# A graph layer and a mixture of experts on one core: search rounds in two of three slots, weight pieces, row copies and first marks moved

## The chip, the cores and the metric

The kernel runs on 1 core of one Trainium2 chip. The metric is the device time of that core in microseconds, launch to end, of one execution. Only the order of the work changes, not what is computed.

## What is computed

The input is x (4096 rows of 128) and a dense float32 matrix adj (4096 by 4096), most of whose entries are 0. In short:

```python
# graph part; n = layernorm(x)
filt = tanh(adj * adj) * (adj > 0)
new_adj = filt with only the 350 largest entries of each row kept
h2 = tanh(n @ W_proj + b_proj)
x = x + relu(new_adj @ (h2 @ W_gcn) + b_gcn)
# expert part; n = layernorm(x), E = 8 experts, the 2 best per row
scores = n @ Wg.T + bg
probs = softmax(the 2 highest scores)
x = x + sum over those 2 experts e of probs * (relu(n @ W1[e].T + b1[e]) @ W2[e].T + b2[e])
```

Hidden width is 512. Only few rows of adj have more than 350 positive entries; the kernel counts the positive entries of every row, corrects up to four rows among the first 512 early on, and has a general repeat for the rest that is skipped when the counts ask for none.

## The kernel before, in words

Each of the five engines (SP, POOL = GpSimd, DVE = VectorE, ACT = ScalarE, PE = TensorE) has a program of its own, written out by hand in the order in which it runs; semaphores join them. An engine that waits holds everything behind the wait.

**The stream.** adj is read in 64 chunks of 1 MB (NCH), eight (NK) for each of the eight blocks of 512 rows of the result (NB, IW). SP issues the loads (line 450) into four buffers; the load of chunk n waits until ScalarE has squared chunk n - 4 and VectorE has marked it (s_sq, s_raw, lines 448 and 449). ScalarE squares (line 1235) and takes tanh (1239), TensorE multiplies with g_sb (1487), VectorE counts positive entries with mark_positive (lines 939 to 950; even chunks write marks, odd ones add). Each engine's program has one slot n for each chunk, 65 in all (FFN). Other work is put into slots by number.

**The start.** VectorE normalises x in eight groups of 512 rows (normal_group, 760), TensorE turns them, projects them, ScalarE applies tanh into g_sb. POOL waits for all eight groups (644), then loads the first four pieces of the expert weights and prepares constants.

**The weights.** W2 and W1 come in eight pieces each. VectorE splits a piece into two float16 halves (split_piece, 959) in the slot that WAT (58) gives. For W1, POOL first loads a piece and its last row (first_pair, 593) and subtracts (take_last_row, line 605); staging has room for two such pairs, so each pair waits for the split of an earlier one. bias_row (690) puts the bias in after the last split.

**The early search.** For up to four rows of block 0 with more than 350 entries the 350th largest value is found in 15 rounds (STEPS), one in each of slots 20 to 34 (STEP0). A round is count_candidates (797) on VectorE, a matmul (1412) on TensorE, and raise_threshold (807) on VectorE in the next slot. Before it a row of flags goes out and back by DMA (1318, 786), the rows are fetched (394) and squared (793). In slot TIE (35) and after, ties are counted and the rows corrected; write_features (836) is in slot 42.

**The routing.** A finished block b = ORDER[i] is routed from slot START[i] on, each step at an offset: add_features (856) at +1, normalise (869) and cut_rows (880) at +2, transposes on TensorE and copy_norm on ScalarE (1276) at +3, the gate and choose (893) at +4, choose_second (905) and exp_diff (1285) at +5, places (1466), probabilities (913) and assign (921) at +6. Then POOL scatters the block's rows to DRAM by expert with eight indirect DMAs (scatter, 697, issue in 709). It waits for the cut, the copy, the probabilities and the assignment. POOL's program has the scatters in order, one behind the other, with no slot numbers.

**The experts.** SP waits for the end of the stream's use of abuf, for the scatters of the first six blocks (516, 517) and for the tile table of first_tiles (1022), which is made in slot FIRST (58); then it loads 256-row tiles by transposing DMAs (469, 471) into abuf. TensorE works on 36 tiles (layer1 and layer2, 1563 and 1581), ScalarE and VectorE in between (1334, 1136, 1342, 1144), POOL scatters the results (727). The blocks i = 6 and 7 are still being routed beside the first tiles; slot 65 is tile 0. At the end the results are read back, added and stored.

## Time and profile before

| | us |
|---|---|
| median of 3 runs | 498.88 |
| lowest, highest | 494.01, 499.02 |
| the profiled execution | 498.55 |
| its span, first to last instruction | 496.8 |
| TensorE busy | 405.6 (82%) |
| VectorE busy | 361.9 (73%) |
| ScalarE busy | 324.0 (65%) |
| POOL busy | 224.5 (45%) |

The stream takes about the first 309 us of the span, the experts the time to about 474, the last reading, adding and storing the rest. The busy shares are averages over these stages; they don't say what sets the end of one. For that one reads a table by stage, and then the waits.

### The profile page before, as it was taken

How to read it: one execution, taken by the hardware profiler on the slowest of the kernel's cores; microseconds unless marked ns; L12 is line 12 of the kernel's file. 1: busy time of each engine (PE TensorE's matmuls, PEld its weight loads, DVE VectorE, ACT ScalarE, POOL GpSimd, SP SyncE). 2: the span in 40 equal slices, each digit the busy share in tenths (PEclk: the TensorE clock that was granted, in tenths of full speed). 3: DMA queues.
4: the chain of work that ended last, by engine and by line, in shares of the span. 5: the costliest groups of instructions: out<-in, count | busy, mean ns of one | idle time of the engine just before them, and what ended most of it. 6: DMA issues, size and time to landing. Idle time of an engine off the chain costs nothing.

```text
span 496.8 us, 7360 instructions
## 1 busy us (share of the span) xinstructions
PE 405.6 (82%) x2144; PEld 232.5 (47%) x2144; DVE 361.9 (73%) x952; ACT 324.0 (65%) x329; POOL 224.5 (45%) x315
## 2 busy tenths in 40 slices
PE   2896999989889899999999999588578779687600
PEld 2453533334434334544554444466357668576500
DVE  4999958678999999969799998296356545354326
ACT  4577999899678879999998995153144344253300
POOL 7249965240217008144054883644744545535510
PEclk9998999989799999999999999888879999988955
DMA  8629889894658568776766982622234333210059
GB/s 277 245 97 413 334 278 324 304 353 150 245 214 252 194 222 296 294 292 240 289 214 239 312 301 49 107 54 56 98 96 88 85 56 78 63 40 30 22 177 335
DMA packets 54898, 97.08 MB, mean 195 GB/s; under 512 B 34165, under 2 KB 41386, under 8 KB 46658
## 3 DMA queue, kind: packets, MB, share of 16 engines
q1 hardware_dynamic: 43584, 79.40, 47.7%
q0 software_dynamic: 6560, 14.88, 9.6%
q10 hardware_dynamic: 4706, 2.23, 1.5%
q8 instruction: 21, 0.34, 0.3%
q14 instruction: 27, 0.22, 0.1%
HBM read 80.00 MB, written 12.27 MB: 186 GB/s over the span
## 4 chain that ended last, share of the span: by engine, by line
PE 43%; DVE 23%; issue 10%; ACT 9%; another core or an unknown queue 7%; DMA 6%; SPq 1%; ACTq 1%; POOL 0%; POOLq 0%; DVEq 0%
PE bank L1487 23%; ACT tbuf L1235 5%; PE bank L1601 5%; DVE marks L950 3%; PE bank L1602 3%; PE bank L1575 2%; PE bank L1577 2%; PE bank L1576 2%; DVE marks L947 2%; DMA tbuf<-expert_rows 2%; DVE rowbf L802 2%; DVE tbuf L1136 2%; DMA xres<-in_x 2%; DVE abuf L1144 1%
## 5 line engine op out<-in xcount | busy, mean ns | idle before, releaser
L1487 PE MATMUL bank<-tbuf,g_sb 128*128 128x512 f32 x512 | 242.4, 619 | 8.3 <-ACT g_sb L1249 5.2
L1487 PEld LDWEIGHTS bank<-tbuf,g_sb 128*128 128x128 f32 x512 | 95.6, 197 | 115.1 <-issue 98.9
L1235 ACT ACTIVATE tbuf<-abuf 128x2048 f32<-128x2048 f32 x64 | 121.5, 1898 | 13.1 <-DMA abuf<-in_adj_tiles 10.4
L1239 ACT ACTIVATE tbuf<-tbuf 128x2048 f32<-128x2048 f32 x64 | 122.3, 1911 | 2.0
L709 POOL DMA_INDIRECT routed_rows<-aug,slots x64 | 79.1, 1236 | 79.9 <-DVE base L930 62.0
L727 POOL DMA_INDIRECT expert_rows<-abuf,xmeta x72 | 70.5, 979 | 73.0 <-DVE abuf L1144 58.5
L950 DVE SCALAR_TENSOR_TENSOR marks<-abuf,marks 128x2048 bf16<-128x2048 int32 x32 | 76.4, 2387 | 1.6 <-DMA abuf<-in_adj_tiles 0.5
L1136 DVE SCALAR_TENSOR_TENSOR tbuf<-bank,tbuf 128x512 f16<-128x512 f32 x72 | 46.9, 682 | 37.2 <-ACT tbuf L1334 19.9
L1601 PE MATMUL bank<-w2hl,tbuf 128*128 x288 | 58.1, 288 | 15.5 <-issue 10.8
L1334 ACT ACTIVATE tbuf<-bank 128x512 f16<-128x512 f32 x72 | 41.0, 605 | 44.7 <-remote 27.3
L1602 PE MATMUL bank<-w2hl,tbuf 128*128 x288 | 54.4, 228 | 8.5 <-issue 8.5
L1342 ACT ACTIVATE abuf<-bank,xmeta 128x128 f32<-128x128 f32 x72 | 23.0, 371 | 53.8 <-remote 33.2
L1144 DVE SCALAR_TENSOR_TENSOR abuf<-bank,xmeta,abuf 128x128 f32<-128x128 f32 x72 | 22.0, 343 | 40.0 <-ACT abuf L1342 34.7
L1575 PE MATMUL bank<-abuf,w1h 128*128 128x256 f16 (+1 forms) x160 | 43.6, 275 | 4.6 <-issue 4.1
L1577 PE MATMUL bank<-abuf,w1l 128*128 128x256 f16 (+1 forms) x160 | 43.6, 275 | 3.5 <-issue 3.5
L1576 PE MATMUL bank<-abuf,w1h 128*128 128x256 f16 (+1 forms) x160 | 43.6, 275 | 1.8 <-issue 1.8
L947 DVE TENSOR_SCALAR marks<-abuf 128x2048 bf16<-128x2048 int32 x32 | 42.9, 1340 | 0.1
L1601 PEld LDWEIGHTS bank<-w2hl,tbuf 128*128 128x128 f16 x288 | 29.5, 103 | 21.8 <-issue 17.2
L1602 PEld LDWEIGHTS bank<-w2hl,tbuf 128*128 128x128 f16 x288 | 29.5, 103 | 14.4 <-issue 14.1
L1575 PEld LDWEIGHTS bank<-abuf,w1h 128*128 x160 | 16.4, 103 | 10.3 <-issue 7.6
L598 POOL DMA_DIRECT2D wstage<-in_w x8 | 5.8, 728 | 32.5 <-DVE w1l L973 32.2
L1577 PEld LDWEIGHTS bank<-abuf,w1l 128*128 x160 | 16.5, 103 | 5.6 <-issue 3.7
(250 smaller groups left out, 438.0 us busy)
## 6 DMA issues: line engine op xcount, KB each, us to landing
abuf<-in_adj_tiles SPq DMA_DIRECT2D x64, 1024.0 KB
wstage<-in_w POOLq DMA_DIRECT2D x24, 256.0 KB, 6.4
tbuf<-expert_rows SPq DMA_DIRECT2D x8, 512.0 KB, 7.2
out<-xres ACTq DMA_DIRECT2D x8, 256.0 KB, 6.2
routed_rows<-pad SPq DMA_DIRECT2D x9, 130.0 KB
expert_rows<-abuf,xmeta POOLq DMA_INDIRECT x72
routed_rows<-aug,slots POOLq DMA_INDIRECT x64
abuf<-routed_rows SPq DMA_TRANSPOSE x40
```

The lines of the kernel that those rows point to most:

```text
L709: pool.indirect_dma_start(xs, bass.IndirectOffsetOnAxis(ap=slots[:, q, k * SUB + cc:k * SUB + cc + 1], axis=0), aug[:, q, k, cc, :], None) ...
L727: pool.indirect_dma_start(ys, bass.IndirectOffsetOnAxis(ap=xmeta[:, t % NT, s, 0:1].bitcast(i32), axis=0), ysb[:, u, s, :], None, bounds_c ...
L950: dve.scalar_tensor_tensor(mark, bits_in, 1.0, mark, ALU.min, ALU.add).then_inc(s_raw, 1)
L1136: dve.scalar_tensor_tensor(hl[:, q, hb, :].rearrange("p h s -> p (h s)"), ps_h(q, half)[:, :], 0.0, hh[:, q, hb, :].rearrange("p h s -> p ...
L1235: act.activation(tbuf[:, n % NBUF, :, :], abuf[:, n % NBUF, :, :], ACT.Square).then_inc(s_sq, 1)
L1239: act.activation(tbuf[:, n % NBUF, :, :], tbuf[:, n % NBUF, :, :], ACT.Tanh).then_inc(s_t, 1)
L1487: last = pe.matmul(ps_feat[ib % 2][:, :], g_sb[:, c, :], tbuf[:, buf, cc, :], start=(c == 0), stop=(c == C - 1))
L1575: pe.matmul(dst, hi, xhl[:, u, 0, rows], start=True, stop=False)
L1576: pe.matmul(dst, hi, xhl[:, u, 1, rows], start=False, stop=False)
L1577: last = pe.matmul(dst, lo, xhl[:, u, 0, rows], start=False, stop=True)
L1601: pe.matmul(y_bank(t, s), hs, hi_lo, start=False, stop=False, skip_group_check=True)
L1602: last = pe.matmul(y_part(t, s, 0), ls, hi, start=False, stop=(hb == HB - 1), skip_group_check=True)
```

## The change

The search runs in two of every three slots from 20 to 41 (SEARCH) instead of in each of 20 to 34, so TIE moves from 35 to 42 and what hangs on it by 7. W1's pieces are split in slots 10, 12, 14, 16, 18 and 44, 46, 48 instead of 11, 13 ... 25; POOL loads the last pair, and puts in the bias row, between the scatters of i = 2 and i = 3. START[4] and START[5] move from 47 and 51 to 50 and 54, and with the latter FIRST from 58 to 61. On ScalarE the copy of the cut rows becomes copy_rows at +5 (it stood with copy_norm at +3), the exponential moves from +5 to +6 and the probabilities from +6 to +7; the last block keeps +3, +5 and +6. The marks of chunks 0 to 3 are made between x's last groups (0 and 1 after group 4, 2 after group 5, 3 after group 6), and POOL's wait for the groups asks for five instead of eight.

```diff
--- before.py
+++ after.py
@@ -55,23 +55,26 @@
     NTA = NT
     PW = 512
     NPC = E * H // PW
-    WAT = [2 + i if i < NPC else 11 + 2 * (i - NPC) for i in range(2 * NPC)]
+    WAT = [2 + i for i in range(NPC)] + [10, 12, 14, 16, 18, 44, 46, 48]
     NCH = NB * NK
 
 
     ORDER = list(range(1, NB // 2 + 1)) + [0] + list(range(NB // 2 + 1, NB))
-    START = [19, 27, 35, 43, 47, 51, 58, 65]
+    START = [19, 27, 35, 43, 50, 54, 58, 65]
 
     AT_ADD, AT_NORM, AT_TURN, AT_COPY, AT_GATE = 1, 2, 3, 3, 4
-    AT_CHOOSE, AT_SECOND, AT_EXP, AT_PLACE, AT_PROB, AT_ASSIGN = 4, 5, 5, 6, 6, 6
+    AT_CHOOSE, AT_SECOND, AT_PLACE, AT_ASSIGN = 4, 5, 6, 6
+
+    AT_ROWS, AT_EXP, AT_PROB = ([s] * (NB - 1) + [e] for s, e in ((5, 3), (6, 5), (7, 6)))
     OUT = 1
     MARKS = 4
     GROUPS = 4
     TOTAL = 3
     FIX = NK + TOTAL + 2
     STEP0 = FIX + 7
-    TIE = STEP0 + STEPS
+    SEARCH = [STEP0 + 3 * b // 2 for b in range(STEPS)]
+    TIE = SEARCH[-1] + 1
     FFN = NCH + 1
 
     COUNT = 14
@@ -641,7 +644,7 @@
             for b in range(STEPS):
                 for k in range(4):
                     pool.memset(bits[:, b, k:k + 1], k << (2 * (STEPS - 1 - b)))
-            pool.wait_ge(s_xn1, NK)
+            pool.wait_ge(s_xn1, NK - 3)
             for i in range(4):
                 load_weights(i)
             pool.memset(pad[:, :, :], 0.0)
@@ -713,12 +716,15 @@
             unit_column()
             first_pair(0)
             first_pair(1)
-            for j in range(NPC):
+            for j in range(NPC - 1):
                 take_last_row(j)
-                if j + 2 < NPC:
+                if j + 2 < NPC - 1:
                     first_pair(j + 2)
-            bias_row()
             for i, b in enumerate(ORDER):
+                if i == 4:
+                    first_pair(NPC - 1)
+                    take_last_row(NPC - 1)
+                    bias_row()
                 if i:
                     scatter(i - 1, routed)
             def store_tile(t, u):
@@ -760,16 +766,6 @@
                     ins = dve.tensor_scalar(xnorm[g % XG][:, c % CK, 0:D - 1], xres[:, c, 0:D - 1], mean[:, c:c + 1],
                                             rstd[:, c:c + 1], ALU.subtract, ALU.mult)
                 ins.then_inc(s_xn1, 1)
-
-            for i, (c0, c1) in enumerate(PIECES):
-                dve.wait_ge(s_x[i], 16)
-                for c in range(c0, c1):
-                    last = dve.bn_stats(stats[:, c, :], xres[:, c, :])
-                link(last)
-                link(norm_scale(dve, link, c0, c1 - c0))
-                for g in range(c0 // CK, c1 // CK):
-                    normal_group(g)
 
             CHAIN = 2 + 4 * STEPS + 1 + 4 + R
             TOTS = STEPS + 1
@@ -1067,10 +1063,10 @@
 
             def ready_steps(n):
 
-                if STEP0 < n <= TIE:
-                    raise_threshold(early, 0, n - STEP0 - 1)
-                if STEP0 <= n < TIE:
-                    count_candidates(early, 0, n - STEP0)
+                if n - 1 in SEARCH:
+                    raise_threshold(early, 0, SEARCH.index(n - 1))
+                if n in SEARCH:
+                    count_candidates(early, 0, SEARCH.index(n))
                 if n == TIE:
                     count_ties(early, 0)
                 for i, b in enumerate(ORDER):
@@ -1087,14 +1083,27 @@
                         cut_rows(i, routed)
                     if n == START[i] + AT_CHOOSE:
                         choose(i, b, routed)
-                    if n == START[i] + AT_PROB:
+                    if n == START[i] + AT_PROB[i]:
                         probabilities(i, routed)
                     if n == START[i] + AT_ASSIGN:
                         assign(i, routed)
+
+            FIRST_MARKS = {NK - 4: (0, 1), NK - 3: (2,), NK - 2: (3,)}
+            for i, (c0, c1) in enumerate(PIECES):
+                dve.wait_ge(s_x[i], 16)
+                for c in range(c0, c1):
+                    last = dve.bn_stats(stats[:, c, :], xres[:, c, :])
+                link(last)
+                link(norm_scale(dve, link, c0, c1 - c0))
+                for g in range(c0 // CK, c1 // CK):
+                    normal_group(g)
+                    for n in FIRST_MARKS.get(g, ()):
+                        mark_positive(n)
+
             for n in range(FFN):
                 ready_steps(n)
-                if n < NCH:
+                if NBUF <= n < NCH:
                     mark_positive(n)
                 for i in range(2 * NPC):
                     if n == WAT[i]:
@@ -1274,11 +1283,13 @@
 
             def copy_norm(i, rs):
-                q = i % 2
                 act.wait_ge(rs.r2, i + 1)
                 if i:
                     act.wait_ge(rs.r3, i)
                 act.activation(xnt[:, :], space(i).xn[:, :], ACT.Copy).then_inc(rs.xt, 1)
+
+            def copy_rows(i, rs):
+                q = i % 2
                 act.wait_ge(rs.cut, 2 * i + 2)
                 act.activation(aug[:, q, 1, :, 0:D], aug[:, q, 0, :, 0:D], ACT.Copy).then_inc(rs.ax, 1)
 
@@ -1295,7 +1306,9 @@
                 for i in range(NB):
                     if n == START[i] + AT_COPY:
                         copy_norm(i, routed)
-                    if n == START[i] + AT_EXP:
+                    if n == START[i] + AT_ROWS[i]:
+                        copy_rows(i, routed)
+                    if n == START[i] + AT_EXP[i]:
                         exp_diff(i, routed)
 
             for n in range(FFN):
@@ -1358,6 +1371,7 @@
                     relu_rows(general, r)
                 for i in range(NB):
                     copy_norm(i, rerouted)
+                    copy_rows(i, rerouted)
                     exp_diff(i, rerouted)
                 for t in range(NT, 2 * NT):
                     relu_h(t, t % 2)
@@ -1487,8 +1501,8 @@
                     last = pe.matmul(ps_feat[ib % 2][:, :], g_sb[:, c, :], tbuf[:, buf, cc, :],
                                      start=(c == 0), stop=(c == C - 1))
                 last.then_inc(s_pe, 1)
-                if STEP0 <= n < TIE:
-                    total_candidates(early, 0, n - STEP0)
+                if n in SEARCH:
+                    total_candidates(early, 0, SEARCH.index(n))
 
             def pair_counts(m):
```

## Rows read from the trace of the kernel before

**Rows 1.** Stages: each engine's busy us (instructions), TensorE's granted clock, DMA share, GB/s.
```profile
60.00:110.00 50.00, 47.27 (x129) 19.27 (x130) 35.22 (x43) 47.01 (x28) 23.50 (x32) 0.97 0.88 312
110.00:190.00 80.00, 72.20 (x243) 33.29 (x242) 74.21 (x199) 64.81 (x42) 20.82 (x22) 0.96 0.63 217
190.00:308.00 118.00, 117.21 (x477) 56.60 (x476) 105.62 (x300) 109.88 (x78) 55.96 (x48) 1.00 0.74 258
...
302.00:304.00 2.00, 2.00 (x6) 0.93 (x6) 1.73 (x9) 1.97 (x2) 0.13 (x1) 1.00 0.35 66
308.00:324.00 16.00, 10.90 (x88) 7.85 (x87) 4.64 (x12) 4.03 (x9) 7.69 (x8) 0.85 0.57 93
```
The columns are PE, PEld, DVE, ACT and POOL in this order.

**Rows 2.** Waits of VectorE from 110 to 308 us: us in total, times, longest.
```profile
DVE scores L895 <- PE bank L1463: 1.9, 2, 1.7
DVE okc L809 <- PE bank L1412: 1.6, 1, 1.6
```

**Rows 3.** Timeline of POOL: start, us, what, idle before it and its releaser.
```profile
31.97 2.59 POOL L590 DMA_DIRECT2D wstage<-in_w  x4 [16.80 <-DVE aug L760]
...
109.98 1.26 POOL L605 TENSOR_TENSOR wstage<-wstage 128x512 f32<-128x512 f32 x1
...
271.62 1.67 POOL L709 DMA_INDIRECT routed_rows<-aug,slots  x1 [5.36 <-DVE base L930]
...
286.88 0.98 POOL L709 DMA_INDIRECT routed_rows<-aug,slots  x1 [0.28 <-POOL aug L701]
...
296.83 1.61 POOL L709 DMA_INDIRECT routed_rows<-aug,slots  x1 [0.30 <-issue]
...
310.91 0.98 POOL L709 DMA_INDIRECT routed_rows<-aug,slots  x1 [8.78 <-DVE base L930]
```

**Rows 4.** Timeline of SP's queue at its first tile load.
```profile
301.11 1.33 SPq L469 DMA_TRANSPOSE abuf<-routed_rows  x1
```

**Rows 5.** Timeline of TensorE at its first tile.
```profile
309.72 0.28 PE L1575 MATMUL bank<-abuf,w1h 128*128 128x256 f16 x1
```

**Rows 6.** Timeline of VectorE: start, us, what.
```profile
28.53 1.10 DVE L760 TENSOR_SCALAR xnt<-xres,moments,rstd 128x127 f32<-128x127 f32 x4
...
110.31 2.02 DVE L947 TENSOR_SCALAR marks<-abuf 128x2048 bf16<-128x2048 int32 x1
...
133.76 0.42 DVE L971 TENSOR_SCALAR w1h<-wstage 128x512 f16<-128x512 f32 x1
...
134.82 0.18 DVE L895 TENSOR_TENSOR scores<-bank,gate_b 128x32 f32<-128x32 f32 x1
...
150.10 0.14 DVE L809 SCALAR_TENSOR_TENSOR okc<-bank,cand 128x4 f32<-128x4 f32 x1
...
151.74 2.28 DVE L950 SCALAR_TENSOR_TENSOR marks<-abuf,marks 128x2048 bf16<-128x2048 int32 x1
...
284.79 0.15 DVE L1018 TENSOR_TENSOR tiles<-base,base_i 1x8 f32<-1x8 f32 x1
...
288.36 2.27 DVE L950 SCALAR_TENSOR_TENSOR marks<-abuf,marks 128x2048 bf16<-128x2048 int32 x1
...
300.86 1.22 DVE L947 TENSOR_SCALAR marks<-abuf 128x2048 bf16<-128x2048 int32 x1
...
305.27 2.29 DVE L950 SCALAR_TENSOR_TENSOR marks<-abuf,marks 128x2048 bf16<-128x2048 int32 x1
```

**Rows 7.** Timeline of ScalarE at the square of chunk 4.
```profile
38.71 1.91 ACT L1235 ACTIVATE tbuf<-abuf 128x2048 f32<-128x2048 f32 x1 [4.26 <-DMA abuf<-in_adj_tiles]
```

**Rows 8.** Waits of VectorE from 40 to 110 us.
```profile
DVE top L786 <- DMA b_f<-key: 3.9, 1, 3.9
DVE rowval L793 <- DMA rowval<-in_adj_rows: 3.1, 1, 3.1
```

**Rows 9.** Chain of waits from 38 to 60 us: start, us, what.
```profile
43.10 3.48 PE bank L1487 x4
...
47.47 1.72 PE bank L1487 x4
```

## The prediction, made before the changed kernel was run

> **What bounds the kernel now.** I read the stages first [rows 1]. From 60 to 110 us ScalarE is busy 47.0 of 50 us and VectorE only 35.2: ScalarE sets the pace. From 110 to 190 VectorE has 74.2 of 80, TensorE 72.2, ScalarE 64.8. From 190 to 308 TensorE shows 117.2 of 118, and VectorE 105.6. That looks as if VectorE had room for more work in the last stretch, but its busy time leaves out the short pauses between linked instructions. So I read its waits next [rows 2]: in the 198 us from 110 to 308 it waits for another engine about 3.5 us in all (1.9 for the gate scores, 1.6 for a count total). VectorE is therefore full from slot 20 to slot 63, and TensorE is nearly full beside it in the second part. A slot is one chunk of the adjacency matrix; its number can be counted off by the marks.
>
> At the hand-over to the experts I read the queues. SP can issue the first tile load only when the scatter of the sixth routed block (i = 5) has landed: the scatter's last issue is at 296.83 and takes 1.61, and SP's first transpose is at 301.11 [rows 3, 4], 2.7 us behind it. TensorE starts the first tile at 309.72 [rows 5], straight after the stream. So the loads are some 5 us ahead of need today, and that cushion is what the change touches.
>
> **The change, part by part.**
>
> *First marks earlier.* Normalising a group takes 1.10 us with a pitch near 1.0 [rows 6]. Chunk 0's mark moves ahead of three groups, so chunk 4's load starts 3 us earlier; ScalarE sat 4.26 us waiting for it [rows 7]. The work of VectorE is only reordered, and TensorE turns group 5 long after it is ready, so the cover holds. POOL's weight loads, which waited 16.80 us until 31.97 for the last group [rows 3], also go 3 us earlier. But what follows passes through a chain with fixed latencies: the flag row is written and read back (VectorE waits 3.9), then four adjacency rows are fetched (3.1) [rows 8]. The key is ready only after slot 13 on VectorE. In slot 10 W1's first piece now stands before the bias: it waits for POOL, which I place 3 us earlier than today, and mark 11 comes some 2 us later than today; slots 11 to 13 make that good, as one split and the bias no longer stand there. I leave 0.7 us of the 3 for the key and all behind it. Bounds: 3 us gained, or 1 us lost if POOL does not come earlier.
>
> *W1's pieces.* One piece costs 134.82 - 133.76 = 1.1 us [rows 6]. The fifth moves from slot 19 to slot 18, into the 3.1 us wait for the rows: 1.1 gained ahead of slot 20. POOL's subtraction at 109.98 ran against mark 20, which took 2.02 where such a mark takes 1.22 [rows 3, 6]: 0.8 gained, as this subtraction now runs in the slack before. The subtraction for the seventh piece leaves the full stretch too; I give it the same 0.8. Pieces six to eight (3.2 us) stay inside the full stretch, only later. On POOL's queue the last pair of loads (two transfers of 256 KB), its subtraction and the bias row's two transfers move behind the scatter of block i = 2 and ahead of that of i = 3, which waits for slot 50 anyway; their 0.5 MB are small beside the 258 GB/s that the stream moves there [rows 1]. The split in slot 48 waits for that subtraction. I expect POOL to be done about 1 us before; if not, VectorE waits one for one, and with it all marks behind.
>
> Here a rule bears on the sum. The row shows 2.02 against 1.22 for the mark beside POOL's subtraction [rows 3, 6]. The Trainium skill ("SBUF — State Buffer", "SBUF: two separate sides") says that VectorE and GpSimd take one port pair as an exclusive lock, and that the loser stands still for the whole instruction. By this rule the same collision comes back wherever the last subtraction lands, and one of the two gains of 0.8 falls away if the moved subtraction meets a mark again: 500.6 instead of 499.8. The trace agrees for this pair.
>
> *Early search.* One round (raise, count) is 151.74 - 150.10 = 1.64 us [rows 6]. Slots 20 to 34 had 15 rounds and now have 10: 8.2 us and with pieces six to eight 11.4 us leave these slots. All of it comes back in slots 35 to 48. As VectorE waits for almost nothing in either part [rows 2], a shift inside a full engine's queue gains nothing by itself. It can gain only the 3.5 us of waits. The bounds are 3.5 gained, and 3.5 lost where rounds and routing now meet TensorE too early. I take 2 gained: TensorE runs ahead more evenly, but a round still needs its chunk's matmuls.
>
> *ScalarE's copies apart.* The row copy and the exponential stand one to two slots later. ScalarE no longer holds its chunks for them; it was not the bound behind slot 20, so nothing by itself. But the probabilities move from +6 to +7, and a scatter waits for them: every scatter but the last starts one slot later. For the first five nobody is waiting. For i = 5 SP is.
>
> *START 47 and 51 become 50 and 54; the tile table with them (58 to 61).* Block i = 5's places were ready in slot 57, and its scatter queued behind i = 4's. Now its probabilities come at the end of slot 61, where before 300.86 stood [rows 6]. The tile table (288.36 - 284.79 = 3.6 us [rows 6]) then lies behind them, not before.
>
> **The sum.** Slot 20 starts at 110.3 - 0.7 - 1.1 - 0.8 = 107.7. From there to the probabilities of i = 5 VectorE has what it did in 300.86 - 110.31 = 190.55, less the table 3.6, less one collision 0.8, less 2 of waits: 184.2, so 291.9. The scatter: today's last one took 298.44 - 286.88 = 11.6; eight times 0.98 and 0.30 is 10.2 at best, and the one before it took 286.88 - 271.62 = 15.3 [rows 3]. I take 11.6, the nearest in place and neighbours: 303.5. Landing and SP's start 2.7: 306.2. Between 302 and 304 the DMA moved 66 GB/s [rows 1], about one tile of 128 KB in 2 us, so the first tile is there about 3 us after SP's start: 309.2, against 309.72 today: 0.5 earlier. VectorE finishes mark 63 at 291.9 + 3.6 + (307.6 - 300.9) = 302.2, where it ended near 307.6, so the stream does end 5 us sooner; but TensorE then stands idle some 6 us. After such a pause it ran at 1.2 GHz: four of the same matmuls took 3.48 us after a pause and 1.72 a moment later [rows 9]. That costs 1.7 (0 to 1.7). Together 1.2 us later at the experts, and the rest of the kernel follows: its scatter of i = 6 now waits for VectorE's first tile (near 313 instead of 310.91 [rows 3]) but has slack before the last loads. The profiled execution took 498.55 us with a span of 496.8; plus 1.2 gives **499.8 us**. Its own time is 0.3 under the median 498.88, so against the median the forecast is +0.9 us, 0.2%: no change. About 1% (5 us) is what this kernel's runs can tell from none, since its three runs spread from 494.01 to 499.02.
>
> **Rivals.**
> *Slower, 505 us.* The scatter of i = 5 becomes the late step. Its place is the end of slot 61; its price is one for one to the first tile. If POOL brings the eighth piece late, or the rounds wait for TensorE, the 2 us of waits do not go; with a scatter of 15.3 instead of 11.6 it is 2 + 3.7 = 5.7 more: 505.5. It decides from the point where the probabilities of i = 5 end after 295.5. For it speaks that a step ahead of SP moved four slots back; against it that VectorE gains 2.6 us before slot 20.
> *Faster, 492 us.* All 3.5 us of waits go (1.5 more), the start keeps 3 us instead of 0.7 (2.3 more), the scatter takes 10.2 (1.4 more), TensorE keeps its clock (1.7): 499.8 - 6.9 = 492.9. Beside it: after the first tiles TensorE is busy only 10.9 of 16 us [rows 1]; if the pause ahead of the experts takes the place of part of these 5.1 us instead of adding to them, 1 to 3 us more go. For it speaks that the work of that stretch is the same and now starts with an idle engine; against it that the scatter of i = 6 and the tile loads still run in it.
> *It doesn't do what it says, 498.5 us.* The early marks gain nothing behind the key chain, the search only changes places in a full queue, and the cushion before the first tile absorbs the later scatter exactly. No step moves the end.
>
> **Chances.** Forecast 0.40 (its own range 495 to 504), nothing moves 0.10, faster 0.30, slower 0.20. The likeliest is 499.8. The range from 492 to 505.5 leaves out the tails beyond either rival's sum, about 2 in 10. Faster by over 1% 0.30, within 1% 0.50, slower 0.20.
>
> **What would show it.** Right: mark 20 near 107.7; mark 35 over 10 us earlier than today, yet the mark of slot 63 only about 5 us earlier; VectorE without waits in between; SP's first transpose near 306 and TensorE idle 5 us or more before its first tile. Wrong: mark 63 earlier by more than 8 us (VectorE was not full); SP starting before 303; a wait of VectorE for POOL's subtraction in slot 48; TensorE's first tile following the stream at once.

## The result, and the profile after

The changed kernel takes 502.31 us (median of 4 runs, 500.72 to 503.01) against 496.44 us of the kernel before in the same session (4 runs, 493.45 to 499.02): the ratio is 1.0116, 95% interval 1.0074 to 1.0157. The forecast was 499.8 us, no change; the change is slower by 1.2%. The number lay in the range, 2.5 us above the forecast. But the call of "no change", which stood for less than 1%, was wrong: the change is slower, clear of noise, and by a little more than that 1%. The profiled execution took 502.0 us with a span of 500.2, 3.4 more than the span before; the medians differ by 5.9.

The page of the changed kernel, its second part (busy tenths in 40 slices of 12.5 us, granted clock) and the chain by engine:

```profile
PE   3999987999999999999999981858648798788500
...
PEclk9999997999999999999999995859959999979955
...
DVE 28%; PE 26%; issue 11%; POOL 10%; DMA 10%; another core or an unknown queue 7%; ACT 4%; SPq 2%; ACTq 1%; DVEq 1%; POOLq 0%
```

Slice 24 of PE (from 300 us) is where a 9 became a 1, and PEclk has a 5 there. That is the hand-over to the experts. The stages of [rows 1] again, from 110 us on, same columns:

```profile
110.00:190.00 80.00, 78.29 (x273) 35.81 (x273) 74.47 (x204) 78.00 (x50) 24.25 (x21) 1.00 0.71 255
190.00:308.00 118.00, 107.73 (x450) 51.91 (x448) 102.38 (x297) 97.07 (x71) 50.91 (x47) 0.98 0.65 229
302.00:304.00 2.00, 0.62 (x4) 0.11 (x4) 1.79 (x6) 0.00 (x0) 1.70 (x2) 0.57 0.10 33
308.00:324.00 16.00, 11.11 (x88) 9.36 (x89) 5.49 (x18) 3.61 (x7) 5.04 (x6) 0.75 0.47 76
```

From 110 to 190 us TensorE is busy 78.3 of 80 us, where it had 72.2: the stream runs ahead. From 302 to 304 it had 2.00 and has 0.62, and from 308 to 324 its mean clock fell from 0.85 to 0.75. In the chain POOL has 10% where the kernel before had 0%, and PE 26% where it had 43%: the scatter, once beside the work, is now part of what sets the end. What was gained in the stream is lost at its end.

VectorE's waits from 40 to 110 us (us in total, times, longest), answering to [rows 8]:

```profile
DVE w1h L967 <- POOL wstage L608: 8.1, 1, 8.1
DVE top L782 <- DMA b_f<-key: 5.7, 1, 5.7
DVE rowval L789 <- DMA rowval<-in_adj_rows: 0.9, 1, 0.9
```

and from 110 to 305, answering to [rows 2]:

```profile
DVE w1h L967 <- POOL wstage L608: 1.9, 1, 1.9
DVE aug L884 <- issue: 1.6, 1, 1.6
DVE okc L805 <- PE bank L1426: 1.5, 3, 0.6
DVE scores L891 <- issue: 1.3, 1, 1.3
DVE feat_t L837 <- issue: 0.5, 1, 0.5
```

The start has a new wait of 8.1 us for GpSimd's first subtraction; a wait of 5.7 us of the bias for TensorE, which the kernel before has at 71.76, is gone. For the full stretch [rows 2] shows only part of the waits of the kernel before. These two belong to it as well:

```profile
DVE feat_t L841 <- issue: 2.9, 1, 2.9
DVE place L924 <- PE bank L1473: 0.8, 1, 0.8
```

So VectorE waited 7.2 us before and waits 6.8 now: nearly the same, yet the stretch is shorter.

The hand-over, engine by engine. VectorE's timeline: the row cut of block i = 6, the probabilities of i = 5, and the last mark of the stream.

```profile
288.70 0.43 DVE L884 CAST aug<-nrm 128x508 f16<-128x508 f32 x1 [1.56 <-issue]
...
292.45 0.17 DVE L915 TENSOR_TENSOR aug<-ex,aug 128x4 f32<-128x4 f32 x1
...
300.12 2.29 DVE L946 SCALAR_TENSOR_TENSOR marks<-abuf,marks 128x2048 bf16<-128x2048 int32 x1
```

POOL's timeline: the moved subtraction, then the first and the last of the eight issues of scatter i = 5.

```profile
232.83 1.27 POOL L608 TENSOR_TENSOR wstage<-wstage 128x512 f32<-128x512 f32 x1 [7.48 <-DMA wstage<-in_w]
...
293.49 0.99 POOL L712 DMA_INDIRECT routed_rows<-aug,slots  x1 [6.93 <-DVE aug L915]
...
304.83 0.97 POOL L712 DMA_INDIRECT routed_rows<-aug,slots  x1 [0.30 <-issue]
```

SP's first transpose, answering to [rows 4]:

```profile
308.46 1.32 SPq L472 DMA_TRANSPOSE abuf<-routed_rows  x1
```

TensorE: the last matmul group of the stream, the first tile's first three matmuls, the second tile's first, answering to [rows 5]:

```profile
302.46 0.62 PE L1518 MATMUL bank<-marks,ones_bf 128*32 128x512 bf16 x4 [1.53 <-DVE marks L946]
311.98 0.39 PE L1589 MATMUL bank<-abuf,w1h 128*128 128x256 f16 x1 [8.90 <-DMA xmeta<-routed_rows]
312.16 0.42 PE L1590 MATMUL bank<-abuf,w1h 128*128 128x256 f16 x1
312.37 0.42 PE L1591 MATMUL bank<-abuf,w1l 128*128 128x256 f16 x1
...
316.30 0.27 PE L1589 MATMUL bank<-abuf,w1h 128*128 128x256 f16 x1
```

Read them as one chain: probabilities end at 292.62, scatter from 293.49 to 305.80, SP at 308.46, first tile at 311.98. TensorE has nothing to do from 303.1 on. Before, the tile stood at 309.72 straight behind the stream. It is 2.3 us later now, and the second tile, at 312.15 before, is 4.15 us later, since TensorE comes back at half clock. The matmuls of the first tile follow each other in 0.21 us; in the kernel before it was 0.11:

```profile
309.84 0.27 PE L1576 MATMUL bank<-abuf,w1h 128*128 128x256 f16 x1
309.95 0.27 PE L1577 MATMUL bank<-abuf,w1l 128*128 128x256 f16 x1
```

The granted clock from 312 to 314 us is 0.50 where it was 1.00, the 1.2 GHz level instead of 2.4.

### The profile page after: what moved, and what is told of

It is laid out like the page before. It is cut to its first block, busy times and chain, and to the rows that moved or that the text cites. A ratio compares the mean times of both kernels' runs of the same rounds, so it can differ in the third digit from the quotient of the medians.

```text
span 500.2 us, 7361 instructions
## 1 busy us (share of the span) xinstructions
PE 401.0 (80%) x2144; PEld 230.2 (46%) x2144; DVE 360.7 (72%) x952; ACT 324.0 (65%) x329; POOL 224.8 (45%) x315
## 4 chain that ended last, share of the span: by engine, by line
DVE 28%; PE 26%; issue 11%; POOL 10%; DMA 10%; another core or an unknown queue 7%; ACT 4%; SPq 2%; ACTq 1%; DVEq 1%; POOLq 0%
PE bank L1501 10%; DVE marks L946 6%; POOL routed_rows L712 6%; PE bank L1615 4%; DVE marks L943 3%; DMA wstage<-in_w 3%; DMA xres<-in_x 3%; PE bank L1591 3%; PE bank L1589 2%; DVE tbuf L1145 2%; DMA tbuf<-expert_rows 2%; PE bank L1590 2%; PE bank L1616 2%; ACT tbuf L1244 2%
## 5 line engine op out<-in xcount | busy, mean ns | idle before, releaser
L1501 PE MATMUL bank<-tbuf,g_sb 128*128 128x512 f32 x512 | 237.7, 610 | 4.2 <-ACT g_sb L1258 2.8
L1501 PEld LDWEIGHTS bank<-tbuf,g_sb 128*128 128x128 f32 x512 | 94.4, 194 | 108.9 <-issue 98.2
L712 POOL DMA_INDIRECT routed_rows<-aug,slots x64 | 81.1, 1267 | 112.3 <-DVE aug L915 76.4
L1615 PE MATMUL bank<-w2hl,tbuf 128*128 x288 | 56.7, 285 | 6.1 <-issue 4.0
L1616 PE MATMUL bank<-w2hl,tbuf 128*128 x288 | 53.6, 227 | 8.6 <-issue 8.5
L943 DVE TENSOR_SCALAR marks<-abuf 128x2048 bf16<-128x2048 int32 x32 | 41.3, 1291 | 0.2
L1589 PEld LDWEIGHTS bank<-abuf,w1h 128*128 x160 | 16.3, 102 | 21.4 <-issue 18.9
L608 POOL TENSOR_TENSOR wstage<-wstage 128x512 f32<-128x512 f32 x8 | 14.3, 1784 | 18.1 <-DMA wstage<-in_w 18.0
```

The lines of the kernel that those rows point to most:

```text
L712: pool.indirect_dma_start(xs, bass.IndirectOffsetOnAxis(ap=slots[:, q, k * SUB + cc:k * SUB + cc + 1], axis=0), aug[:, q, k, cc, :], None) ...
L943: dve.tensor_scalar(mark, bits_in, 1.0, None, ALU.min).then_inc(s_raw, 1)
L1501: last = pe.matmul(ps_feat[ib % 2][:, :], g_sb[:, c, :], tbuf[:, buf, cc, :], start=(c == 0), stop=(c == C - 1))
L1589: pe.matmul(dst, hi, xhl[:, u, 0, rows], start=True, stop=False)
L1615: pe.matmul(y_bank(t, s), hs, hi_lo, start=False, stop=False, skip_group_check=True)
L1616: last = pe.matmul(y_part(t, s, 0), ls, hi, start=False, stop=(hb == HB - 1), skip_group_check=True)
```

## The experiments

There are twelve runs, in three groups; each ratio is against runs of the kernel before beside it. The first two groups ran on chips on which the kernel before takes 450 us, the last on one where it takes 497. Up to the first tile the timelines agree between them to about 2 us; the difference lies in the experts' phase (last section). So ratios are compared throughout, and times of the trace up to the first tile.

"Mark n" is the start of VectorE's mark of chunk n. Each such time comes from one execution, and executions of the same code differ: the six traces with the changed kernel's start have mark 20 between 108.55 and 110.46. A difference of less than 2 us between two traces proves little; the ratios rest on more executions.

### The anchors

**changed_again**: the changed kernel, unedited.

> The changed kernel, nothing edited, on the chip of the other runs of this group: the anchor for them. The hand-over theory expects the same timeline up to the hand-over as in its first profile (mark 63 near 300, SP's first transpose near 308.5, first tile near 312) and slower than the kernel before by 1 to 1.5%. If the loss belonged to the experts' phase of the first chip, where 14 tiles took 45 us longer than here, it would now be within 0.5% of the kernel before.

Measured: ratio 1.0121 [1.0086, 1.0156]. Mark 63 at 299.49, SP at 307.97, first tile at 311.83, span 454.3. The loss is the same 1.2% on a chip whose experts' phase is 47 us shorter, so it doesn't come from what is particular to the first chip.

**before_again**: the kernel before, unedited.

> The kernel before, nothing edited, on the same chip, for its trace: mark 63 near 305, SP's first transpose near 301, first tile near 309.7 or, if this chip's stream ends earlier, straight after it; its time is that of the kernel before.

Measured: ratio 0.9993 [0.9969, 1.0017], span 448.7. Mark 63 at 306.66, SP at 303.32, first tile at 311.12 straight behind the stream.

These two traces are the cleanest pair. Stages of the kernel before (columns as in [rows 1]), then of the changed one:

```profile
300.00:311.00 11.00, 11.00 (x42) 5.22 (x40) 9.11 (x23) 6.37 (x7) 3.37 (x3) 1.00 0.26 48
311.00:318.00 7.00, 7.00 (x71) 6.31 (x68) 4.74 (x11) 3.85 (x9) 4.48 (x5) 1.00 0.60 104
```

```profile
300.00:311.00 11.00, 0.70 (x8) 0.10 (x4) 3.16 (x6) 0.00 (x0) 4.77 (x5) 0.63 0.14 36
311.00:318.00 7.00, 6.17 (x35) 5.08 (x36) 1.81 (x5) 1.79 (x3) 0.71 (x1) 0.60 0.43 75
```

and TensorE's first and second tile in each, before first:

```profile
311.12 0.28 PE L1575 MATMUL bank<-abuf,w1h 128*128 128x256 f16 x1
...
313.54 0.27 PE L1575 MATMUL bank<-abuf,w1h 128*128 128x256 f16 x1
```

```profile
311.83 0.39 PE L1589 MATMUL bank<-abuf,w1h 128*128 128x256 f16 x1 [9.61 <-DMA xmeta<-routed_rows]
...
316.50 0.29 PE L1589 MATMUL bank<-abuf,w1h 128*128 128x256 f16 x1
```

The first tile is only 0.71 us later (311.83 against 311.12), but the second follows after 4.67 instead of 2.42: 2.25 us for half clock. Counting the tiles on, tile 24 starts 4.3 us later (387.7 against 383.4) and the span ends 5.6 us later. Of the 4.3 us only 0.7 are thus the later start. TensorE's mean clock from 310 to 418 us is 0.95 instead of 1.00: it is at half level in the first tile and again behind the gap that follows the fourth (granted clock 0.50 from 327 to 330 us, 1.00 in before_again, which has a gap there too). Why it falls in that gap in one kernel and not in the other is open. The last 1.3 us, behind the last tile, I can't name.

### The hand-over by itself

**before_block5_late**, on the kernel before:
```
-    START = [19, 27, 35, 43, 47, 51, 58, 65]
+    START = [19, 27, 35, 43, 47, 55, 58, 65]
```


> The kernel before, with block i = 5 started at slot 55 instead of 51, so that its probabilities stand in slot 61, where the changed kernel has them; nothing else differs. Theory A (the hand-over sets the start of the experts): TensorE's stream still ends near 308, but the scatter of i = 5 starts behind slot 61 (about 301 us), ends near 313, SP's first transpose comes near 316 and the first tile near 319 instead of 309.7: 505 to 508 us, slower by 6 to 9. Rival B (the loss lies in the search or in the later W1 pieces, and the cushion takes the late scatter): within 2 us of the kernel before.

Measured: 1.0352 [1.0325, 1.0379], 15 us. SP's queue, then TensorE's last group of the stream and its first tile:

```profile
319.70 1.32 SPq L469 DMA_TRANSPOSE abuf<-routed_rows  x1
```

```profile
314.99 0.40 PE L1504 MATMUL bank<-marks,ones_bf 128*32 128x512 bf16 x4 [1.44 <-DVE marks L950]
323.65 0.39 PE L1575 MATMUL bank<-abuf,w1h 128*128 128x256 f16 x1 [8.26 <-DMA xmeta<-routed_rows]
```

The cushion doesn't take the late scatter. Block i = 5's probabilities end at 304.1 here, and the first tile is 19.6 us behind. The cost was larger than expected (6 to 9): the probabilities came 3 us later than I had put them, so the first tile is 12.5 us later than in before_again (323.65 against 311.12), and the pause of 8.3 us adds its clock. VectorE's mark 63 came at 312.65 instead of 306.66, which I had not expected. Its waits tell where that comes from: from 110 to 315 us it waits 16.0 us for TensorE and the features' copy, where it waited 8.7 in before_again, and what came on top are waits for TensorE. The longest is 4.25 us for the gate's scores, at 290.89; in before_again its longest wait for TensorE is 1.8:

```profile
290.89 0.19 DVE L895 TENSOR_TENSOR scores<-bank,gate_b 128x32 f32<-128x32 f32 x1 [4.25 <-PE bank L1463]
```

Why TensorE has these results later was not traced.

**block5_one_slot_sooner**, on the changed kernel:
```
-    START = [19, 27, 35, 43, 50, 54, 58, 65]
+    START = [19, 27, 35, 43, 50, 53, 58, 65]
```


> The changed kernel with block i = 5 started at slot 53 instead of 54 and nothing else. Theory A: one slot is 4 us here, so the scatter ends near 302, SP starts near 304.5 and the first tile comes near 308: 3 to 4 us less, 498 to 499. Rival B: the block only changes places, same as the changed kernel within 1 us.

Measured: 1.0022 [0.9997, 1.0047], against 1.0121 of the changed kernel: 1% back, 4.5 us, as the hand-over says. SP at 303.60, first tile at 307.24; mark 63 (300.13) hasn't moved. One digit takes back the loss, up to the 0.5% that the interval leaves. Rival B is out.

**copies_together_again**, on the changed kernel:
```
-    AT_ROWS, AT_EXP, AT_PROB = (... ((5, 3), (6, 5), (7, 6)))
+    AT_ROWS, AT_EXP, AT_PROB = (... ((3, 3), (5, 5), (6, 6)))
```


> The changed kernel with ScalarE's row copy, exponential and the probabilities back at +3, +5 and +6 for every block; thin search and late blocks stay. Theory A: the probabilities of i = 5 stand one slot sooner (60), scatter ends near 302, first tile near 308: 3 to 4 us less than the changed kernel, as with block 5 one slot sooner. Rival B (ScalarE then holds its chunks back and TensorE's stream with them): mark 63 1 to 3 us later and the gain halved or gone.

Measured: 1.0005 [0.998, 1.0029], 1.2% back. SP at 302.52, first tile at 306.48, TensorE still waits 6.9 us for it. Mark 63 stands at 296.82, 2.7 us earlier than in the changed kernel, so this trace shows no sign that ScalarE's copies inside the chunks' way hold the stream back (rival B wanted it later). Part of that, 1.7 us, was there at mark 20 already (108.55 against 110.21), where nothing is edited.

**search_dense_again**, on the changed kernel:
```
-    START = [19, 27, 35, 43, 50, 54, 58, 65]
+    START = [19, 27, 35, 43, 47, 51, 58, 65]
-    SEARCH = [STEP0 + 3 * b // 2 for b in range(STEPS)]
+    SEARCH = [STEP0 + b for b in range(STEPS)]
```


> The changed kernel with the search back at one round per slot and the blocks i = 4 and 5 back at slots 47 and 51; early marks, W1's late pieces and the copies apart stay. Theory A: the probabilities of i = 5 come in slot 58, its scatter ends near 301, SP starts near 304, and the first tile follows the stream near 308 to 310: 497 to 499 us, 3 to 5 under the changed kernel. Rival B (W1's late pieces or the one-slot-later probabilities cost by themselves): stays at 501 to 503. Rival C (the thin search is what shortened the stream by 5 us): mark 63 ends near 305 again instead of 300.

Measured: 0.996 [0.9935, 0.9985]. The first tile (305.56) comes 3.6 us behind SP's first transpose and only 0.6 behind the stream. Mark 63 is at 300.99, where rival C wanted 305 and the changed kernel has 299.49: most of the stream's gain is not the thin search's. Blocks 4 and 5 moved in the same edit, so the two parts are not told apart here. No cost of W1's late pieces shows either.

The chain from the probabilities to the first tile can now be read from six traces in which TensorE waited for it over 4 us:

| kernel | probabilities of i = 5 end | SP's first transpose | first tile | sum |
|---|---|---|---|---|
| changed, first profile | 292.6 | 308.5 | 312.0 | 19.4 |
| changed_again | 292.0 | 308.0 | 311.8 | 19.8 |
| before_block5_late | 304.1 | 319.7 | 323.7 | 19.6 |
| block5_one_slot_sooner | 288.7 | 303.6 | 307.2 | 18.6 |
| copies_together_again | 285.1 | 302.5 | 306.5 | 21.4 |
| w1_odd_slots (below) | 290.0 | 306.0 | 309.5 | 19.6 |

(The last column is the distance from the probabilities to the first tile.) In copies_together_again the scatter alone, from its first issue to the end of its last, took 13.3 us, against 12.3 in the first profile. The first tile comes at the later of two: 18.6 to 21.4 us behind these probabilities, mostly 19 to 20, or the end of the stream.

### The start

**w1_odd_slots**, on the changed kernel:
```
-    WAT = [2 + i for i in range(NPC)] + [10, 12, 14, 16, 18, 44, 46, 48]
+    WAT = [2 + i for i in range(NPC)] + [11, 13, 15, 17, 19, 44, 46, 48]
```


> The changed kernel with W1's first five pieces back in slots 11, 13, 15, 17 and 19 instead of 10, 12, 14, 16 and 18. VectorE waited 8.1 us in slot 10 for GpSimd's first subtraction, so the theory that this wait ate what the early marks gained expects it to fall to about 5 us, mark 13 near 78 instead of 81 and mark 20 up to 1 us earlier or, with a piece in slot 19 and a collision beside mark 20, 1 us later. The hand-over theory expects the end to follow the probabilities of i = 5 one for one: within 1.5 us of the changed kernel either way. The rival (the start decides on its own) expects 3 us less.

Measured: 1.0105 [1.0079, 1.0132]. Mark 20 at 107.69; on the same chip two kernels with the changed kernel's start have it at 110.46 (block5_one_slot_sooner) and 108.96 (search_dense_again). First tile at 309.51, 2.3 earlier than in changed_again. The time's interval can't be told from the changed kernel's. VectorE's timeline here (bias, mark 11, W1's first piece, mark 13), then the changed kernel's:

```profile
65.41 0.28 DVE L974 TENSOR_SCALAR b_f<-bank 32x128 f32<-32x128 f32 x1
...
66.18 2.27 DVE L946 SCALAR_TENSOR_TENSOR marks<-abuf,marks 128x2048 bf16<-128x2048 int32 x1
74.20 0.43 DVE L967 TENSOR_SCALAR w1h<-wstage 128x512 f16<-128x512 f32 x1 [5.75 <-POOL wstage L608]
...
77.19 4.01 DVE L946 SCALAR_TENSOR_TENSOR marks<-abuf,marks 128x2048 bf16<-128x2048 int32 x1
```

```profile
73.78 0.43 DVE L967 TENSOR_SCALAR w1h<-wstage 128x512 f16<-128x512 f32 x1 [8.06 <-POOL wstage L608]
...
74.85 0.27 DVE L974 TENSOR_SCALAR b_f<-bank 32x128 f32<-32x128 f32 x1
...
75.61 2.27 DVE L946 SCALAR_TENSOR_TENSOR marks<-abuf,marks 128x2048 bf16<-128x2048 int32 x1
...
81.08 2.28 DVE L946 SCALAR_TENSOR_TENSOR marks<-abuf,marks 128x2048 bf16<-128x2048 int32 x1
```

The piece can be split at about 74 in both, because GpSimd's transfers and subtraction decide. With the piece in slot 10 the bias and mark 11, 3.1 us of work that needs nothing from GpSimd, queue behind the wait; with it in slot 11 they fill it. So mark 13 is at 77.2 instead of 81.1.

The other traces agree on mark 13 and less on what is left at mark 20. With the changed kernel's slots mark 13 stands at 80.6 to 81.5 (six traces), with slots 11, 13 and so on at 77.2 to 77.4 in three; a fourth, milder_search_copies_together, has 79.7, but its first mark was 2.4 us late already (29.20 against 26.79 in milder_search). At mark 20 it is 108.6 to 110.5 against 107.7 to 108.0 and, in the late trace, 110.66: 0.6 to 2.8 us, not 2.8 for certain.

**early_marks_alone**, on the kernel before (the old loop over x's pieces goes):
```
-            pool.wait_ge(s_xn1, NK)
+            pool.wait_ge(s_xn1, NK - 3)
...
+            FIRST_MARKS = {NK - 4: (0, 1), NK - 3: (2,), NK - 2: (3,)}
...
+                    for n in FIRST_MARKS.get(g, ()):
+                        mark_positive(n)
...
-                if n < NCH:
+                if NBUF <= n < NCH:
```


> The kernel before with only the early marks (chunks 0 to 3 marked between x's last groups, and the weight loads' wait three groups earlier). W1's order stays 11, 13, 15 and so on. By the prediction's step 0.7 us are left of three: first tile 0.7 earlier, within 0.3% of the kernel before. The runs so far (mark 20 at 107.7 to 107.9 with W1 in odd slots, 111.4 in the kernel before) say that over 2 us are left when the first piece of W1 does not wait: mark 20 near 108.5 to 109.5, first tile 2 to 3 us earlier, ratio 0.993 to 0.997.

Measured: 0.9949 [0.9919, 0.9978]. Mark 20 at 109.14 (110.31 in [rows 6]), mark 63 at 302.38 instead of 305.27, first tile at 306.84, 2.9 us earlier than in the first profile; the ratio says 2.5, with 1.1 to 4.0 in its interval. The early marks, together with the earlier weight loads, keep most of the 3 us of which I had left 0.7. At mark 20 only 1.2 us of it show; at mark 35 it is 2.9 (186.71 against 189.59 in the first profile). What gave the rest between the two was not looked into.

### The clock in the pause

**pause_filled**, on the changed kernel, ahead of the experts' tiles on TensorE:
```
+            for _ in range(42):
+                pe.matmul(bank[0][:, :], ones_bf[:, :], marks[:, 0, 0, :], start=True, stop=True)
```


> The changed kernel with 42 idle matmuls (128x512, their result is never read) on TensorE between its stream and the first tile, so that the pause of 9.6 us is filled without moving anything else. Theory: the granted clock stays at full, the first tile is followed by the second 2.4 us later as in the kernel before, where the changed kernel took 4.7, and the time falls by 2 to 3.5 us to 452 to 453.5, so that the pause costs its clock beside its length. Rival: the late loads set the second tile as well, and nothing moves.

Measured: 1.0097 [1.0061, 1.0133]; not told apart from the changed kernel. TensorE:

```profile
302.86 11.18 PE L1659 MATMUL bank<-marks,ones_bf 128*128 128x512 bf16 x42
313.88 0.27 PE L1589 MATMUL bank<-abuf,w1h 128*128 128x256 f16 x1
...
316.29 0.27 PE L1589 MATMUL bank<-abuf,w1h 128*128 128x256 f16 x1
```

The pitch to the second tile is 2.4 us instead of 4.3, as expected. But the idle matmuls ran partly at half clock themselves (granted clock 0.50 from 303 to 306 us, 0.86 from 306 to 309), took 11.2 us and ended about 2 us after the tile could have started: SP's first transpose was at 308.21, and the tile follows it by 3.5 in the first profile. Second tile at 316.29 against 316.30: the clock costs some 2 us at the second tile, and they are paid either way here. That a pause without this cost would also end the kernel earlier, the other half of the theory, this run doesn't show; my count of 42 was too high.

### Both gains without the loss

**dense_search_and_odd_w1**: search_dense_again with w1_odd_slots's line.

> The changed kernel with both undone: search one round per slot with blocks 4 and 5 at slots 47 and 51, and W1's first five pieces in slots 11, 13, 15, 17, 19. Early marks, W1's last three pieces late and the copies apart stay. Theory A (the first tile sets the end, and the two gains add up): mark 20 near 107 instead of 109, scatter of i = 5 ends near 297, first tile at the end of the stream near 303: 2 to 3 us under the dense search alone, 5 to 6 under the kernel before, 1.2%. Rival (the W1 order gains only where VectorE is the late one, and the stream of TensorE ends at the same time): as the dense search alone, 0.4% under the kernel before.

Measured: 0.9918 [0.9891, 0.9944]. Scatter i = 5 ends at 298.3, SP at 300.92, first tile at 304.46, 1.1 us earlier than in search_dense_again. The time is 0.4% (1.9 us) below that kernel's, where 2 to 3 us were expected, and the two intervals just overlap: that the gains add up is likely, but not clear of noise.

**milder_search**, on the one before:
```
-    SEARCH = [STEP0 + b for b in range(STEPS)]
+    SEARCH = [STEP0 + 5 * b // 4 for b in range(STEPS)]
```


> Built on dense_search_and_odd_w1: the search in four of five slots (20 to 37) instead of every slot, blocks 4 and 5 at 47 and 51. VectorE waited 3.2 us for the features' copy and 1.3 for the places with the dense search, which the thin one did not show. Theory: these waits go in part, mark 63 comes near 298.5 instead of 300, the first tile near 303 instead of 304.5, 1 to 1.5 us less: 444 to 445, ratio 0.987 to 0.991. Rival: the search only changes places in a full queue and the time stays at that of dense_search_and_odd_w1, 445.4.

Measured: **0.9829** [0.9786, 0.9873], 488.01 us where the kernel before takes 496.69. Mark 63 at 295.42 and TensorE without a pause:

```profile
298.87 0.62 PE L1518 MATMUL bank<-marks,ones_bf 128*32 128x512 bf16 x8
299.89 0.28 PE L1589 MATMUL bank<-abuf,w1h 128*128 128x256 f16 x1 [0.40 <-DMA xmeta<-routed_rows]
...
302.31 0.27 PE L1589 MATMUL bank<-abuf,w1h 128*128 128x256 f16 x1
```

That is better than the theory had it (mark 63 near 298.5). A search thinned just so far that it ends before slot 38 keeps block i = 4 at slot 47, and with it i = 5 at 51. The wait of 3.2 us for the features' copy is gone, as expected; the 1.3 for the places stayed. How much of the step from 0.9918 to 0.9829 is the search's stays open: the two ran on different chips, and dense_search_and_odd_w1 was not repeated on this one.

**milder_search_copies_together**: the same with the copies as in copies_together_again.

> milder_search with ScalarE's row copy, exponential and the probabilities back at +3, +5 and +6 for every block. Theory: the scatter of i = 5 starts one slot sooner, so SP is not late in any case, and the stream of VectorE alone sets the first tile: as milder_search or up to 1.5 us less (443 to 445). Rival: with the copies in the chunks' way ScalarE holds TensorE back and the stream ends 1 to 2 us later.

Measured: 0.9822 [0.9782, 0.9862], no different from milder_search. The trace looks otherwise: mark 63 at 299.82, first tile at 304.06, 4.2 us later than in milder_search. Of these 2.4 are there at the first mark, ahead of every edit; the other 1.8 are what the rival wanted (1 to 2 us), but the ratios don't show them, and their intervals are too wide to rule them out. So no effect of ScalarE's copies apart is shown once the hand-over isn't late, and milder_search's own 299.89 is the value of one execution, and one below the median (486.76 against 488.01). Both versions beat the two kernels.

## Why the prediction was right in part, and where it failed

*The start, 2.6 us earlier at mark 20 (107.7).* Wrong: 109.92, 0.4 earlier. One part is a slip in the sum: the collision of 0.8 lies inside mark 20, behind its start, so it belongs to the stretch that follows, and the mark should have been put at 108.5. The 291.9 isn't changed by it. Of the other terms, the early marks by themselves were undersized (0.7 was left; 1.2 at mark 20 and 2.9 at the first tile in early_marks_alone). I saw that the piece in slot 10 stands ahead of the bias and waits for GpSimd, and wrote that slots 11 to 13 make that good. They don't: one slot later, mark 13 comes 3.2 us or more earlier, and of this 0.6 to 2.8 are left at mark 20 (w1_odd_slots). So the rows for the search were ready at 105.17, 0.2 later than before, where I had them 0.7 earlier. The "1.1 gained" by the fifth piece was half there: from mark 19 to mark 20 it is 4.5 us instead of 5.1.

*The subtraction's collision.* With W1 in even slots it did go: mark 20 takes 1.22 instead of 2.02. That was partly luck, as before_block5_late, with the old slots, has 1.22 there too. The rule that I weighed against it is that of the Trainium skill ("SBUF — State Buffer", "SBUF: two separate sides"): VectorE and GpSimd hold one port pair in turn, and the loser stands still. Its size fits these pairs. In w1_odd_slots mark 13, from 77.19 on, took 4.01 us instead of 2.28 beside this row of POOL,

```profile
77.76 1.28 POOL L608 TENSOR_TENSOR wstage<-wstage 128x512 f32<-128x512 f32 x1
```

The mark ended at 81.20, which is, to 0.1, its usual 2.28 us behind the end of that row (79.04). By the same section of the Trainium skill the one that starts first gets the ports. Here the mark's row starts first and loses, so who wins can't be told from the starts of these rows. In the changed kernel it was GpSimd's subtraction that took 2.67 instead of 1.27 at 106.13, beside a mark of normal length; in its time one small instruction of VectorE (at 108.18) took 0.64 instead of 0.15, so half a us of the 0.8 came back ahead of mark 20. The moved subtraction met no mark at 232.83; VectorE waited 1.9 us for it instead, in slot 48, the sign of a wrong step that I had named. Cost: those 1.9 us, one for one, where I had hoped for POOL 1 us ahead.

*Search spread, 2 us of waits gained.* The stretch came out near the forecast, but not for this reason. From mark 20 to the end of the probabilities VectorE took 182.7 us, where I had 184.2. The 3.5 us of waits that I let the search gain from were a misreading, as the kernel before waits 7.2 there; and of those only 0.4 went. Of the 7.9 us by which the stretch shortened the table is 3.6, the marks are 1.4 (42 of them took 74.0 us instead of 75.4), the waits 0.4, and some 2.5 I can't name. That they stand in for the 2 of the forecast is luck. How much the thinning itself gives stays open too: dense and thin differ by 1.5 us at mark 63 with the start of the changed kernel, 300.99 against 299.49, and milder_search did best of all.

*The hand-over, first tile at 309.2.* This is the step that failed. It was to come 0.5 us earlier than before, and came 2.3 later. Probabilities 0.7 later than forecast (292.6), 0.9 until the scatter's first issue, for which I had no term, scatter 12.3 instead of 11.6, landing 2.66 as forecast, SP to tile 3.5 instead of 3: 2.8 us, and the tile stood at 312.0. Each was small, and none fell on the other side; for the scatter I had taken the lower of the two that the trace offered (11.6 and 15.3). VectorE's wait of 1.6 us at 288.70, for scatter i = 4 (pushed back by START 50) to give its rows free, lies on this chain too.

*The clock.* 1.7 forecast; 1.9 and 2.25 measured at the first tile. But I had it over there. It comes again behind the fourth tile, and in the pair of changed_again and before_again 4.3 us stand at tile 24.

*The slower rival.* It named the place and the price (one for one) rightly, but the forecast's own sum went through the same place. What it added for itself came true in part: the eighth piece was late (1.9 us) and the waits didn't go, but the stretch was no longer for it, and the scatter took 12.3 and not 15.3. So its 505.5 was 3.5 too high against the profiled 502.0, and the forecast 2.2 too low. Its deciding point, probabilities after 295.5, was wrong: with 19.4 us from there to the tile, and about 2 for the clock, anything after 288 us loses against the tile at 309.72. The probabilities at 291.9, as I forecast them, were already 3.6 us behind it. I should have turned the chain around, from the tile needed to the latest start, before giving a chance of 0.20. The faster rival's condition, the whole 3 us of the start, is nearly true of the early marks alone, but not of what was put behind them.

## What to carry to other kernels

Ahead of a phase that is started by a long chain (here 19 us of scatter, landing and load), count back from the first instruction of the phase to the latest moment at which the chain may start, and let nothing push its start behind that moment, however much room the engines seem to have. When a stream in front of such a hand-over is shortened, the chain must come forward by as much, or the gain turns into a pause, and TensorE's clock with it. A wait that is moved on a queue is judged by the independent work that it is moved in front of.

## What the runs showed of the hardware beyond the question

The kernel before takes 496.4 us on the chip of the result, 496.7 on that of the third group, and 450 on the two others. From the first tile to the last of 36 it needs 153.6 us (309.7 to 463.3) there and 106.3 (311.1 to 417.4) here. In the first profile TensorE waits for its own issue in this phase; two rows of its waits from 310 to 470 us, kernel before:

```profile
PE bank L1601 <- issue: 10.8, 11, 2.1
PE bank L1602 <- issue: 8.5, 12, 1.4
```

With the other lines' it is 29.9 us in all, of the 47 us of difference; the trace of before_again shows no such row. The stream in front is the same on both. What slows the issue was not tried; the ratios of the changed kernel (1.0116 and 1.0121) agree all the same.
